# A 16-row transpose widened to 128 rows and columns at the start of a LoRA and top-2 MoE kernel

## What is computed

```python
# first layer, added to x
out = jnp.einsum('btc,oc->bto', x, W_base) + b_base
h = jnp.einsum('btc,erc->bter', x, As)          # 8 experts of rank 16
lora = jnp.einsum('bter,eor,be->bto', h, Bs, w)  # w = cond_8
x = x + out + lora * 2.0
# second layer, added to x
w, sel = top_k(softmax(cond_8), 2); w = w / w.sum()
y = sum over the two chosen experts: w_e * down_e(gelu(gate_e(x)) * up_e(x))
y = y + shared_down(gelu(shared_gate(x)) * shared_up(x))
x = x + y
```

## Time and profile before

| what | us |
|---|---|
| median of 3 runs | 130.63 |
| lowest and highest | 130.32, 130.80 |
| profiled execution, its own time | 131.27 |
| its span, first to last instruction | 129.6 |
| PE busy in the span | 124.8 (96%) |
| DVE, ACT, POOL busy | 90.7, 72.1, 62.4 |

### The profile page before, as it was taken

The page is one execution under the profiler, slowest core; times in us unless marked ns, Lnnn a source line. Parts: engine busy times, 40 slices in busy tenths (PEclk is TensorE's granted clock), DMA queues, the critical chain, the costliest instruction groups (busy, mean ns, idle before and its releaser), DMA issues.

```text
span 129.6 us, 3162 instructions
## 1 busy us (share of the span) xinstructions
PE 124.8 (96%) x873; PEld 113.9 (88%) x873; DVE 90.7 (70%) x177; ACT 72.1 (56%) x136; POOL 62.4 (48%) x111
## 2 busy tenths in 40 slices
PE   6999999999999989999999999999999999999991
PEld 5956977878878858999999999999999999999990
DVE  2696798769979999633377758767777677766641
ACT  2259767976876768113466485657565756611110
POOL 5455964645797947453344632653365513610000
PEclk9999999999999999999999999999999999999999
DMA  3997788599400086579745586558799950013921
GB/s 53 286 337 272 191 289 295 189 260 291 117 3 0 14 249 225 166 273 415 291 190 228 230 326 248 207 200 324 253 311 313 390 190 0 3 33 135 285 66 53
DMA packets 14524, 26.56 MB, mean 205 GB/s; under 512 B 2224, under 2 KB 7600, under 8 KB 12976
## 3 DMA queue, kind: packets, MB, share of 16 engines
q1 hardware_dynamic: 14192, 26.35, 60.5%
q10 hardware_dynamic: 320, 0.07, 0.2%
HBM read 12.52 MB, written 1.31 MB: 107 GB/s over the span
## 4 chain that ended last, share of the span: by engine, by line
PE 93%; DVE 2%; issue 1%; ACT 1%; DVEq 0%; ACTq 0%
PE bank L1049 11%; PE bank L1085 9%; PE bank L1086 9%; PE bank L1087 9%; PE bank L1067 6%; PE bank L996 5%; PE bank L998 5%; PE bank L997 5%; PE bank L1107 5%; PE bank L1108 4%; PE bank L1109 4%; PE bank L1012 3%; PE bank L920 3%; PE bank L928 3%; PE bank L895 3%; PE bank L1013 2%
## 5 line engine op out<-in xcount | busy, mean ns | idle before, releaser
L556 ACT ACTIVATE work<-bank 128x512 f32<-128x512 f32 x48 | 28.7, 599 | 39.8 <-PE bank L1087 17.2
L714 DVE TENSOR_TENSOR bank<-bank,work 128x512 f32<-128x512 f32 x40 | 27.9, 698 | 18.5 <-PE bank L1087 13.0
L731 DVE TENSOR_TENSOR hT_lo<-bank,hT_hi 128x512 fp32r<-128x512 f32 x40 | 27.3, 681 | 1.0 <-issue 0.5
L483 POOL TENSOR_TENSOR wstd<-wexd,wstd 128x512 fp32r<-128x512 f32 x12 | 15.6, 1298 | 24.3 <-ACT wstd L598 24.3
L1085 PE MATMUL bank<-xp,wst 128*128 128x256 f32 x96 | 27.2, 284 | 0.0
L1086 PE MATMUL bank<-xp,wst 128*128 128x256 f32 x96 | 27.2, 283 | 0.0
L1087 PE MATMUL bank<-xp,wst 128*128 128x256 f32 x96 | 27.2, 283 | 0.0
L565 ACT CAST hT_hi<-bank 128x512 fp32r<-128x512 f32 x40 | 23.3, 582 | 1.6 <-DVE bank L714 1.6
L1086 PEld LDWEIGHTS bank<-xp,wst 128*128 128x128 f32 x96 | 18.4, 192 | 0.0
L1085 PEld LDWEIGHTS bank<-xp,wst 128*128 128x128 f32 x96 | 18.4, 192 | 0.0
L1087 PEld LDWEIGHTS bank<-xp,wst 128*128 128x128 f32 x96 | 18.4, 192 | 0.0
(11 more groups left out here) (153 smaller groups left out, 214.9 us busy)
## 6 DMA issues: line engine op xcount, KB each, us to landing
wst<-wex SPq DMA_DIRECT2D x12, 1024.0 KB, 4.8
raw_ex<-n_L_cond_skill_gate_dram SPq DMA_DIRECT2D x8, 256.0 KB, 3.2
raw_ex<-in_L_cond_skill_up_dram SPq DMA_DIRECT2D x8, 256.0 KB, 4.2
sst<-n_L_cond_skill_gate_dram SPq DMA_DIRECT2D x8, 256.0 KB, 3.4
sst<-in_L_cond_skill_up_dram SPq DMA_DIRECT2D x8, 256.0 KB, 4.3
xn<-in_x_dram SPq DMA_DIRECT2D x4, 256.0 KB, 4.5
out_dram<-xT SPq DMA_DIRECT2D x4, 256.0 KB, 2.7
sst<-_L_cond_shared_gate_dram SPq DMA_DIRECT2D x1, 256.0 KB, 4.9
```

Of the source, the lines that this page charges most:

```text
L556: act.activation(gelu_sb[q], gate_ps[q][:, :], ACT.Gelu_apprx_tanh).then_inc(gelu_done, 1)
L714: dve.tensor_tensor(up_ps[u][:, :], up_ps[u][:, :], gelu_sb[q], ALU.mult).then_inc(h_done, 1)
L731: dve.tensor_tensor(hT_lo[:, q, :], up_ps[u][:, :], f32(hT_hi[:, q, :]), ALU.subtract).then_inc(lo_done, 1)
```

## The change

`cond_er`, an array of its own with 16 rows, is gone. In its place `cond_full` is the last 128x128 slot of `xT`. DVE sets it to zero right behind `zeros`, waits for both, and writes the spread conditioning values in its upper 16 rows. The transpose takes all 128 rows, the whole identity, and writes 128 columns of `bank[5]` where it wrote 16. DVE reads the first 16 of them as before. The order of the instructions on PE is the same, and DVE has one instruction more, the second MEMSET.

```diff
-        cond_er = sb("cond_er", [B, E, R])
+        cond_full = xT[:, B - 1, :]
@@ DVE
             dve.memset(zeros[:, :], 0.0).then_inc(zeros_ready, 1)
+            dve.memset(cond_full, 0.0).then_inc(zeros_ready, 1)
+            dve.wait_ge(zeros_ready, 2)
 
             dve.wait_ge(ld_cond, 16)
-            dve.tensor_scalar(cond_er[:, :, :], cond_sb[:, :].rearrange("b (e a) -> b e a", a=1).to_broadcast([B, E, R]),
+            dve.tensor_scalar(cond_full[0:B, :].rearrange("b (e r) -> b e r", e=E), cond_sb[:, :].rearrange("b (e a) -> b e a", a=1).to_broadcast([B, E, R]),
                               LORA_SCALING, None, ALU.mult).then_inc(cond_er_ready, 1)
@@ PE
             pe.wait_ge(cond_er_ready, 1)
-            pe.transpose(bank[5][:, 0:B], cond_er[:, :, :].rearrange("b e r -> b (e r)"), ident[0:B, 0:B]
-                         ).then_inc(setup_ps, 1)
+            pe.transpose(bank[5][:, 0:P], cond_full, ident[:, :]).then_inc(setup_ps, 1)
```

## The result

The changed kernel took 130.74 us in the median (130.63 to 131.24, 18 runs), the kernel before, timed beside it, 130.50 us (130.26 to 130.84, 18 runs). The ratio is 1.0022 with a 95% interval of 1.0014 to 1.0031. So the change costs about 0.29 us by the ratio and 0.24 by the medians: inside what the prediction called within 0.5%, but a loss that is real, where "no change" was forecast.

What follows compares the result with a forecast made beforehand. PE's own pace was taken to bound the kernel. The terms summed 0.00 + 0.00 + 0.00 (0.00 to +0.14 us), so the forecast was no change, 130.6 us, with a range of 129.9 to 131.2.

Steps and rivals of the forecast that it cites:

- What bounds the kernel: Whole kernel: PE, busy 124.8 of 129.6 us, bounds it; an edit counts only by what it changes in PE's queue.
- The added MEMSET: 0: DVE at the start: the 0.17 us MEMSET and the wait behind it lie inside 1.58 us of idle time: 0.
- It keeps its 0.21 us: 0: DVE's spreading of the conditioning values, behind the added wait: waits for the transfer anyway, keeps shape and duration: 0.
- The transpose: +0.00, no gain possible: PE at L901: the 128x128 transpose takes 0.21 us like the 16-row one: +0.00, at most +0.14 us.
- a gain has no row: PE at L901: +0.00 is also the lower bound, because the full-size neighbour isn't faster than the small transpose.
- +0.09 us: PE at L901: counter-estimate from the skill's rule that the gap grows with moving columns, 112 more at 1.2 GHz.
- No slack at `x_transposes(1)`: PE at 7.72 us: it waits for DVE's `wT`, so a longer transpose slot passes to the end in full, +0.14 at most.
- (B): Rival at PE's start: the wide transpose raises the clock sooner; gain capped at 0.8 us, 129.8 us; chance 0.12.
- (A): Rival at the transpose: its slot on PE grows with the columns, +0.14 us, 130.8 us; chance 0.22.
- (C): Rival behind 7.6 us on PE: the clock rises later, about +1.1 us, 131.7 us; chance 0.11.

Runs made afterwards that it cites:

- experiment 5: Kernel before, with two more one-element MEMSETs on DVE behind the one of `zeros`: 130.99 us, ratio 1.0030.
- experiment 2: Changed kernel with DVE's two waits in the other order, the transfer first, then the zeros: 130.70 us, ratio 1.0007.
- experiment 1: Changed kernel with only the transpose put back to 16 rows and columns, second MEMSET and its wait kept: 131.00 us, ratio 1.0033.
- experiment 3: Kernel before, with POOL's third sum of x1 made to wait for DVE's `two_b`: 130.44 us, ratio 0.9996.
- experiment 7: Kernel before without two redundant waits of DVE (`consts` ahead of `wT`, bias ahead of the first split): 130.98 us, ratio 1.0030.
- experiment 9: Experiment 8 with the narrow transpose, so without the zeroing and its wait: 130.12 us, ratio 0.9974.
- experiment 10: Kernel before, unchanged, profiled again for a second trace: one execution of 130.54 us.
- experiment 11: Kernel before, unchanged, profiled again for a third trace: one execution of 130.71 us.
- experiment 4: Changed kernel, with POOL's third sum of x1 made to wait for DVE's `two_b`: 130.13 us, ratio 0.9964.
- experiment 8: Changed kernel with the transfer's wait first, POOL's sum behind `two_b`, and the router's weights behind the first `w_eff`: 129.56 us, ratio 0.9924.
- experiment 6: Changed kernel without two redundant waits of DVE (`consts` ahead of `wT`, bias ahead of the first split): 130.18 us, ratio 0.9976.

## Why the prediction was wrong

**What bounds the kernel.** Right: PE is the chain nearly throughout. But "an edit can move the time only by what it adds to or takes from PE's queue" was the wrong conclusion. The chain of before itself leaves PE between 41.7 and 46.3 us, and I read only its first 12 us. That the time ended inside the range of 129.9 to 131.2 is luck: two terms that the sum put at nothing, of opposite sign, nearly cancel.

**The added MEMSET: 0.** The 0.17 us are hidden, as said. The step that failed is that the wait and the MEMSET were priced at 0, by their time alone, where they stand. Two instructions more in DVE's program cost 0.43 us (experiment 5, with two MEMSETs of one element): 20 us later a pause no longer keeps POOL back, and the price comes due at 43 us. The sum left this term out altogether. The section on the change counted one instruction more; the trace has two.

**"It keeps its 0.21 us: 0".** The duration is kept, the start isn't. In the trace the wait for the zeros hangs on the instruction and the transfer's wait stands ahead of it as an instruction of its own. The values landed at 2.81 and the spreading started at 2.92, 0.11 us behind; in experiment 2, with the waits the other way round, they landed at 2.61 and it started at 2.63, 0.02 behind, as in the kernel before (2.70, 2.72). So the order of the waits costs 0.09 us. The landing itself varies by more, from 2.46 to 2.86 over all traces.

**The transpose: +0.00, no gain possible.** Wrong in sign. I wrote that "a gain has no row". It had: the 0.22 us of idle time before the weight load of L901, which I put down to the conditioning values although the row says "issue", and the 0.22 us from it to the next load. The load starts at 3.20 or 3.21 in every trace of the narrow transpose (the kernel before and experiments 1, 3, 5, 7, 9, 10 and 11, whatever the start of the spreading, 2.62 to 2.85 us). With 128 rows it starts at 2.90 and 2.96 where the spreading started at 2.57 and 2.63 (experiments 4 and 2). That the narrow load waits for the matmul ahead, whose recorded end is 3.28, is my reading and isn't shown. `b_nat` comes at 4.13 in place of 4.43: -0.30 us in place of +0.00, and -0.05 in the changed kernel's own trace, where the values were late. The Trainium skill, "TensorE: Matmul & The Clock Gate", section on what happens when you issue a matmul, says that weight loads are pulled ahead of matmuls in flight when their row groups don't conflict or when the load goes to the background weight buffer, and that the number of rows doesn't matter for a load's time. The trace agrees with the second in the load's own 0.18 us, for 16 rows and for 128. With the first it agrees in that the load behind the wide transpose starts 0.03 to 0.16 us after the transpose's own (3.25 and 3.28, 2.96 and 3.06, 2.90 and 3.06); behind the narrow one it is 0.21 or 0.22 us in every trace. The +0.09 us that the prediction took from the Trainium skill's rule on the gap by columns isn't borne out. The rows of the load and the columns of the matmul were changed together, so which of the two makes the difference wasn't tested.

**No slack at `x_transposes(1)`.** Right in the main: what `b_nat` gains comes through, 4.13 gives 7.37 in experiment 2 and 7.26 in experiment 4, against 7.66 and 7.67 in the two later traces of before. Those two wait for `wT`; the first trace, which I read, shows no wait there, its start at 7.72 is set by PE's own slower pair of `delta_w`. Also right in (B) was that an early clock is capped there. In experiment 4 the four transposes at 4.75, held up by 0.27 us until x had landed (a limit that (B) didn't have), take 0.66 us, as those at 7.26 do, so by their pace TensorE is at 2.4 GHz already, and PE then waits for `wT`:

```profile
7.26 0.66 PE L914 MATMUL bank<-ident,xn 128*128 128x128 f32 x4 [0.65 <-DVE wT L699]
```

**The rivals.** (A), a longer slot, fell, although its sign is there: the changed kernel's chain has 0.45 us for the transpose. But the four instructions behind it take 0.85 in place of 1.15, so the two pieces are 1.30 us against 1.36. That the end is near its 130.8 is luck, for another reason. (B) and (C), the clock: nothing ties the clock to the transpose. The pair of `delta_w` shows the rise late in a wide version (1.56 us, experiment 8) and earlier in narrow ones (1.26, before; 0.86, experiment 9), and it is earliest in a wide one (experiment 4). That wasn't tested by itself. The case that came true, two engines meeting later because the program had moved, wasn't on the list.

## What to carry to other kernels

Where a kernel's tail depends on which of two engines reaches a shared resource first, the cost of an added instruction isn't at its place; look through the whole trace for small operations that last much longer than their size allows and end together with one of another engine, and order them by a wait. To judge such a change, add two empty instructions to the kernel before as a control: here that alone moved the time by 0.43 us, more than the whole change. And a small matmul among full ones can cost more of TensorE's time than a full one in its place, as here.

## What the runs showed of the hardware

- **Some operations of DVE and POOL exclude each other.** A DVE operation on 16 integers took 0.95 to 1.18 us when POOL's sum of two 128x512 arrays had started before it, always ending with it, and 0.17 us when it was first by 0.02 us. DVE's split of 128x512 took 1.79 us in place of 0.68 when POOL's sum was first, and POOL's sum 1.82 in place of 1.27 when it wasn't. DVE operations that read a bank of PE's results and one array run beside POOL's sum at their usual time (`hT_lo`, 0.68 us at 43.20 in experiment 10). The Trainium skill, "SBUF — State Buffer", section on the two separate sides, calls the port pair of the two an exclusive lock that the first to start holds for its whole instruction; on DVE's side it names operations in a two-port mode, or with two SBUF inputs against a POOL operation that reads SBUF. The rows agree: `two_b` and the split have two SBUF inputs, `hT_lo` has one.
- **A pause in DVE's program.** Some 0.43 us (1.12 against 0.69 us of idle time), at the same operation in all six traces with the old length (before, experiments 3, 6, 9, 10, 11), and in none of the seven that are two longer or shorter (after, experiments 1, 2, 4, 5, 7, 8). What it is wasn't tried and stays open; the traces show only that it goes with the place in the program, and that it falls into idle time elsewhere is inferred.
- **The 16-row weight load of this kernel isn't taken ahead.** With the conditioning values spread at the same time (2.62 and 2.63 us), it started at 3.20 (experiments 7, 9 and 11) where the 128-row one started at 2.96 (experiment 2), and the load behind it followed after 0.22 us in place of 0.10. At 1.2 GHz, by the pace, that put the transpose of `b_nat` 0.30 us later.
